# A graph layer and an expert layer in one kernel: wide products, ranks behind bursts, last scatters behind gathers, relation counts standing three times

## The reference

```
h   = layernorm(x)
red = segment_sum(h[src] + relvectors[edge_type], dst)
x   = x + gru_cell(red, h)          # gates r, z, n: 3 x 256 columns of w_ih and of w_hh
y   = layernorm(x)
top two of (y @ Wg + bg) pick experts; each: gelu(y @ W1 + b1) @ W2 + b2
x   = x + sum over the two picked experts
```

## Time and profile before

| | |
|---|---|
| median of three runs | 1621.61 us (1618.15 to 1624.96) |
| profiled execution, its own time | 1622.94 us |
| its span | 1621.1 us, mean granted TensorE clock 0.891 |
| busy: TensorE / its weight loads | 1343.6 us (83%) / 1159.2 us (72%) |
| busy: VectorE / ScalarE / POOL | 1093.0 (67%) / 707.3 (44%) / 1033.3 us (64%) |

### The profile page before, as it was taken

One profiled execution on the slowest core, in us unless ns is written; L12 is line 12 of the kernel. 1 busy time (PEld: TensorE's weight loads), 2 busy tenths in 40 slices (PEclk: granted clock), 3 DMA queues, 4 the chain that ended last, 5 costly groups with the idle time before them and its releaser, 6 DMA issues. The chain is left out here.

```text
span 1621.1 us, 39990 instructions
## 1 busy us (share of the span) xinstructions
PE 1343.6 (83%) x14228; PEld 1159.2 (72%) x14228; DVE 1093.0 (67%) x3967; ACT 707.3 (44%) x1538; POOL 1033.3 (64%) x948
## 2 busy tenths in 40 slices
PE   1169999999999999998898887775754799999991
PEld 1137787888878878777777776664644699999991
DVE  7856677777777777788888888943545555555550
ACT  6323344445455454443443332221212567776660
POOL 2177667677777776677777767777772255555552
PEclk8559999999999999999998998686766899999996
DMA  9676434444454554444444543346641465555556
GB/s 305 171 219 188 143 98 115 128 137 141 138 148 144 144 141 135 129 133 136 134 128 135 147 125 111 111 118 232 211 115 51 102 97 93 93 95 100 95 80 178
DMA packets 136167, 220.59 MB, mean 136 GB/s; under 512 B 27761, under 2 KB 101046, under 8 KB 134688
## 3 DMA queue, kind: packets, MB, share of 16 engines
q0 software_dynamic: 63872, 123.12, 31.1%
q1 hardware_dynamic: 72096, 94.84, 19.5%
HBM read 169.05 MB, written 57.76 MB: 140 GB/s over the span
## 5 line engine op out<-in xcount | busy, mean ns | idle before, releaser
L667 POOL DMA_INDIRECT ring<-h_table,idx x728 | 725.1, 996 | 328.0 <-issue 252.7
L780 ACT ACTIVATE amat<-P 128x300 f16<-128x300 f32 (+3 forms) x608 | 230.9, 427 | 434.9 <-PE P L1635 427.9
L1648 PE MATMUL P<-hs,amat 128*126 128x256 f16 (+4 forms) x2646 | 366.9, 287 | 0.0
L1648 PEld LDWEIGHTS P<-hs,amat 128*126 128x126 f16 (+4 forms) x2646 | 299.7, 140 | 7.1
L721 POOL DMA_INDIRECT out_rows<-yo,xrows x112 | 176.8, 1578 | 162.2 <-DVE yo L1520 110.6
L1136 DVE TENSOR_SCALAR cone<-iota,comb 128x294 f16<-128x294 f16 (+3 forms) x840 | 255.5, 307 | 0.0
L1135 DVE TENSOR_SCALAR lone<-iota,slo 128x128 f16<-128x128 f16 x840 | 221.4, 264 | 32.8 <-PE P L1630 32.4
L1630 PE MATMUL P<-cone,lone 128*128 128x294 f16 (+3 forms) x840 | 164.6, 291 | 41.4 <-ACT amat L780 27.3
L1511 DVE SCALAR_TENSOR_TENSOR gl<-gT,scales,gh 128x512 f16<-128x512 f32 x112 | 84.1, 751 | 127.0 <-ACT gh L904 127.0
L676 POOL DMA_INDIRECT expert_rows<-xrow,slots x100 | 122.5, 1225 | 58.1 <-DVE slots L1265 28.2
L1863 PE MATMUL P<-xh,w_all 128*128 128x256 f16 x896 | 157.8, 275 | 0.0
(11 more groups left out here) (239 smaller groups left out, 2661.8 us busy)
## 6 DMA issues: line engine op xcount, KB each, us to landing
raw<-in_L_ffn_W_dram SPq DMA_DIRECT2D x32, 512.0 KB
xrows<-expert_rows SPq DMA_DIRECT2D x56, 257.0 KB, 3.3
ring<-h_table,idx POOLq DMA_INDIRECT x728
w_parts<-parts SPq DMA_DIRECT2D x16, 512.0 KB, 6.5
w_all<-w_parts SPq DMA_DIRECT2D x8, 1024.0 KB, 19.1
h_in<-h_table SPq DMA_DIRECT2D x25, 250.0 KB
x<-in_x_dram SPq DMA_DIRECT2D x25, 250.0 KB
out_rows<-x SPq DMA_DIRECT2D x25, 250.0 KB
```

What stands on the lines that cost most here:

```text
L667: nc.gpsimd.indirect_dma_start(out=ring[:, r, j, :], out_offset=None, in_=h_dram, in_offset=bass.IndirectOffsetOnAxis(ap=idx[:, slot, g * ...
L780: nc.scalar.activation(amat[:, b % 2, :, s * aw:(s + 1) * aw], P[2 + g % 2][:, 0:HIS * aw].rearrange("p (h w) -> p h w", w=aw), ACT.Copy). ...
L1648: nc.tensor.matmul(to, amat[:, b % 2, hi, 0:used], hs[:, hi, part * D:(part + 1) * D], start=(hi == 0 and part == 0), stop=False)
```

## The change

- `relations`: a new tile `rel_rows` holds the three parts under each other (48 partitions); `onetype` and `ramp` hold the 16 types three times, so that counts and `cts` have 48 rows; 2 matmuls of 48 partitions stand for 6 of 16. SP fills `rel_rows` with 3 small DMAs, queued behind the load of the first `x1` and ahead of the `raw` loads; TensorE waits for them (`s_stack`) before its slot matmuls.
- `head_piece`: one matmul of 512 columns per row block for two of 256; high and low sums lie side by side, and `low_sums` adds the second half with one more operation.
- TensorE's list: `gate_hn`, `transpose_x2` and `rank` go behind the pieces and bursts of their half. ScalarE's `move_group` of the later bursts goes ahead of `high_x2`.
- POOL's list: no scatter is placed behind a step from 88 on. Of the 25 tiles only tile 21 changes its place: from behind step 89 to behind all gathers.
- Start: `group_f` is made ahead of the `comb` operations, the wait for the slot matmuls (`head_slots`) comes at the end of half 0, and `weight_max` starts two halves later. Two tiles swap their places in SBUF.

```diff
-        onetype = sb("onetype", [128, 2, SC, R], F16)
-        cts = sb("cts", [R, STEP_G * WIN], F16)
+        onetype = sb("onetype", [128, 2, SC, PARTS * R], F16)
+        cts = sb("cts", [PARTS * R, STEP_G * WIN], F16)
...
-            return h - 1 if 1 <= h <= WJOBS else None
+            return h - 3 if 3 <= h <= WJOBS + 2 else None
...
             sp.dma_start(x1[:, :, :], node_rows(x, 0)).then_inc(x_loaded, 16)
+            sp.wait_ge(s_parts, 1)
+            for part in range(PARTS):
+                sp.dma_start(rel_rows[part * R:(part + 1) * R, :], rels[:, part, :]).then_inc(s_stack, 16)
...
-                    while done < TILES and (BEGIN[done] + 11) // 2 + 2 <= n:
+                    while n < NS - 3 and (BEGIN[done] + 11) // 2 + 2 <= n:
...
+                    for g in groups_of(h)[len(bursts[0]):] if bursts else []:
+                        move_group(g)
                     for i in stage_of(h, 8):
                         high_x2(i)
-                    for g in groups_of(h)[len(bursts[0]):] if bursts else []:
-                        move_group(g)
...
-                nc.vector.tensor_tensor(s_l[0:used, :], P[1 + 3 * (b % 2)][0:used, 0:D], s_h[0:used, :], ALU.subtract).then_inc(a_low, 1)
+                link(nc.vector.tensor_tensor(s_l[0:used, :], P[1 + 3 * (b % 2)][0:used, 0:D], s_h[0:used, :], ALU.subtract))
+                nc.vector.tensor_tensor(s_l[0:used, :], P[1 + 3 * (b % 2)][0:used, D:PD], s_l[0:used, :], ALU.add).then_inc(a_low, 1)
...
-                for part in range(PARTS):
-                    for f in range(KT):
-                        nc.tensor.matmul(P[0][:, f * STEP_G * WIN:(f + 1) * STEP_G * WIN], rels[:, part, f * 128:(f + 1) * 128],
-                                         cts[:, :], start=(part == 0 and f == 0), stop=False)
+                for f in range(KT):
+                    nc.tensor.matmul(P[0][:, f * STEP_G * WIN:(f + 1) * STEP_G * WIN], rel_rows[:, f * 128:(f + 1) * 128],
+                                     cts[:, :], start=(f == 0), stop=False)
...
-                    for part in range(2):
-                        nc.tensor.matmul(to, amat[:, b % 2, hi, 0:used], hs[:, hi, part * D:(part + 1) * D],
-                                         start=(hi == 0 and part == 0), stop=False)
+                    nc.tensor.matmul(both, amat[:, b % 2, hi, 0:used], hs[:, hi, :], start=(hi == 0), stop=False)
...
+                pe.wait_ge(s_stack, 16 * PARTS)
                 pe.wait_ge(s_groups, 16 * (len(ZONES) + 1) + 1)
...
                     if bursts:
                         head_burst(bursts[0])
-                    for i in stage_of(h, 8):
-                        transpose_x2(i)
-                    for i in stage_of(h, 11):
-                        rank(i)
                     if s == 0 and n < NS:
                         sums(n)
...
-                    for i in stage_of(h, 1):
-                        gate_hn(i)
...
                         if m + 1 < len(bursts):
                             head_burst(bursts[m + 1])
+                    for i in stage_of(h, 1):
+                        gate_hn(i)
+                    for i in stage_of(h, 8):
+                        transpose_x2(i)
+                    for i in stage_of(h, 11):
+                        rank(i)
```

More of the change, by code:

```diff
@@ L256, in shape_constants @@
     ident = np.eye(128, dtype=np.float32)
-    ramp = np.tile(np.concatenate([np.arange(WIN), np.arange(R), np.zeros(128 * len(WIDTHS))]).astype(np.float32), (128, 1))
+    ramp = np.tile(np.concatenate([np.arange(WIN), np.tile(np.arange(R), PARTS), np.zeros(128 * len(WIDTHS))]).astype(np.float32), (128, 1))
     for n, aw in enumerate(WIDTHS):
-        ramp[:, WIN + R + 128 * n:WIN + R + 128 * (n + 1)] = np.arange(128)[None, :] // aw == np.arange(128)[:, None]
+        ramp[:, WIN + PARTS * R + 128 * n:WIN + PARTS * R + 128 * (n + 1)] = np.arange(128)[None, :] // aw == np.arange(128)[:, None]
     iota = np.tile(np.arange(IOTA).astype(np.float16), (128, 1))
@@ L300, in gnn_ffn_kernel @@
         ident16 = sb("ident16", [128, 128], F16)
-        ramp = sb("ramp", [128, WIN + R])
+        ramp = sb("ramp", [128, WIN + PARTS * R])
         iota = sb("iota", [128, IOTA], F16)
@@ L310, in gnn_ffn_kernel @@
         rels = sb("rels", [R, PARTS, D], BF16)
+        rel_rows = sb("rel_rows", [PARTS * R, D], BF16)
         wg = sb("wg", [128, KT, NE])
@@ L428, in gnn_ffn_kernel @@
         with ExitStack() as early:
-            to_slots = early.enter_context(nc.sbuf_tensor("to_slots", [GMAX, len(WIDTHS), 128], F32))
+            slo_i = early.enter_context(nc.sbuf_tensor("slo_i", [128, HEAD * GC], I16))
         cone = sb("cone", [128, BUFS, IOTA], F16)
@@ L436, in gnn_ffn_kernel @@
         acc = sb("acc", [128, KT, ACOLS])
+        with ExitStack() as early:
+            to_slots = early.enter_context(nc.sbuf_tensor("to_slots", [GMAX, len(WIDTHS), 128], F32))
         s_h = sb("s_h", [128, D], F32R)
@@ L530, in _ @@
             load_chunk(1)
-            sp.dma_start(to_slots[:, :, :], c_ramp[0:GMAX, WIN + R:].rearrange("p (w s) -> p w s", s=128)).then_inc(s_const, 16)
-            for to, a in ((ident, c_ident), (ramp, c_ramp[:, 0:WIN + R]), (iota, c_half[:, 0:IOTA]), (cols, c_cols[:, 0:NCOL])):
+            sp.dma_start(to_slots[:, :, :], c_ramp[0:GMAX, WIN + PARTS * R:].rearrange("p (w s) -> p w s", s=128)).then_inc(s_const, 16)
+            for to, a in ((ident, c_ident), (ramp, c_ramp[:, 0:WIN + PARTS * R]), (iota, c_half[:, 0:IOTA]), (cols, c_cols[:, 0:NCOL])):
                 sp.dma_start(to[:, :], a).then_inc(s_const, 16)
@@ L1105, in head_keys, with head_slots @@
                 for first, end, k, aw, size, c in zone_batches():
-                    r = slice(GC * first, GC * end)
-                    nc.vector.scalar_tensor_tensor(comb[:, r], comb[:, r], aw / 128.0, dst_t[:, r], ALU.mult, ALU.add)
                     ins = nc.vector.tensor_copy(group_f[0:size, c], group_i[0:size, c])
                 ins.then_inc(s_groups, 1)
+                for first, end, k, aw, size, c in zone_batches():
+                    r = slice(GC * first, GC * end)
+                    ins = nc.vector.scalar_tensor_tensor(comb[:, r], comb[:, r], aw / 128.0, dst_t[:, r], ALU.mult, ALU.add)
+                link(ins)
+            def head_slots():
                 dve.wait_ge(s_slots, 1)
@@ L1354, in fast @@
                         second_norm(i, ORDER[i])
+                    if h == 0:
+                        head_slots()
                     if pass1_at(h) is not None:
                         weight_max(pass1_at(h))
-                    if h == WJOBS + 1:
+                    if h == WJOBS + 3:
                         weight_tops()
-                    if h == WJOBS + 2:
+                    if h == WJOBS + 4:
                         weight_diag()
-                    if h == WJOBS + 3:
+                    if h == WJOBS + 5:
                         weight_scales()
@@ L1644, in head_piece @@
                         pe.wait_ge(a_added, b - 1)
+                both = P[1 + 3 * (b % 2)][0:used, :]
                 to = P[1 + 3 * (b % 2)][0:used, 0:D]
                 for hi in range(HI * (n * of + m) // (pieces * of), HI * (n * of + m + 1) // (pieces * of)):
-                    for part in range(2):
-                        nc.tensor.matmul(to, amat[:, b % 2, hi, 0:used], hs[:, hi, part * D:(part + 1) * D],
-                                         start=(hi == 0 and part == 0), stop=False)
+                    nc.tensor.matmul(both, amat[:, b % 2, hi, 0:used], hs[:, hi, :], start=(hi == 0), stop=False)
                 if n == pieces - 1 and m == of - 1:
```

20 lines of the change are left out of this document (10 added, 10 removed).

## The result

| | before | after |
|---|---|---|
| median of six runs | 1622.43 us (1618.15 to 1624.96) | 1613.63 us (1612.56 to 1622.13) |
| ratio to before, 95% interval | | 0.9954 [0.9931, 0.9976] |
| first / last gather issued | 72.0 / 1211.2 us | 73.4 / 1208.5 us |
| first slot matmul | 81.1 us | 96.4 us |

Faster by 0.46%, less than the 0.5% that the prediction took as the least to tell from no change, but with an interval that stays under 1; 1604 had been forecast. All ratios leave out executions over 1.5% above the fastest of their kernel, medians in us don't.

The account below looks back on a forecast made before the run. TensorE was taken to set the pace in most steps, POOL near steps 58 to 65 and 76 to 90; -11 - 6 + 2 - 7 + 4 + 1 - 6 + 5 = -18 us gave 1604 us, range for 8 in 10 1588 to 1627.

Parts of the forecast that it names:

- The premise, "a saving per step counts some 63 times": Gather stage: TensorE sets the pace in steps 1 to 57 and 66 to 74, so savings count 63 times, not 91.
- Relations, -11: TensorE's relation matmuls, 2 for 6: four starts fewer save 0.175 us a step, times 63, -11 us.
- Wide products, -6: TensorE's products, 512 columns for twice 256: 5.5 ns saved per pair, some 1130 pairs that count, -6 us.
- VectorE, +2: VectorE's larger onetype (+0.27 us a step) and one more 0.41 us operation in 27 batches: 0 to +8, +2 taken.
- Order, -7 + 4: TensorE's list: waits for h_l, mask and xrow shrink, -7 us (0 to -15); new slot waits cost +4 (0 to +17).
- Scatters, +1: POOL's list: later ranks make slots later for scatters; +1 us taken.
- the slower rival: POOL's scatters wait for later ranks and stop the gathers behind them, giving 1630 us; chance 0.15.
- Tail, -6: End of POOL's list: tile 21's four scatters go behind all gathers, so the last gather goes out earlier, -6 us.
- Start, +5: Slot matmuls wait for rel_rows, landing about 95 us, 14 us late; most is made good, +5 us taken.

Follow-up runs that it names:

- e16: Kernel after without the low half of the gathered rows in the products, 16 matmuls of 48 columns a step instead of 32: 1608.43 us, 0.9887 of before.
- e13: Kernel after, unchanged, run again as the yardstick: 1618.06 us, 0.9942 of before.
- e17: e14 with TensorE's and ScalarE's lists in the order of the kernel before: 1620.93 us, 0.9969 of before.
- e18: e17 with each burst's products as two matmuls of 256 columns again, without VectorE's extra addition per batch: 1618.17 us, 0.9951 of before.
- e15: Kernel after with each wide product split into four matmuls of 128 columns: 1633.84 us, 1.0043 of before.
- e14: Kernel after with the three copies into rel_rows issued early on ScalarE's queue instead of SP's: 1610.52 us, 0.9889 of before.

## Why the prediction was wrong, by its steps

- **The premise, "a saving per step counts some 63 times".** This is the step that failed. It took POOL's stops for proof that TensorE paces steps 1 to 57. e16 is the test: 0.4 us less per step, 37 us in all, give 9.6, where the premise has 26. TensorE is the pace of a step only until VectorE and ScalarE are. From e13 to e16 TensorE's idle time in steps 10 to 90 grew from 130 to 143 us, as waits for `amat`, `cone` and slots, and its time at the lower clock from 181 to 212 us, half of which is lost: 13 + 15 is about what didn't arrive. The change itself shows the same: steps 10 to 59 take 625.9 us before, 640.0 in after and 633.6 in e13. They gave nothing back, though TensorE's relations take 0.16 us less in each of them.
- **Relations, -11.** The saving on TensorE is real (0.16 us a step, 0.175 forecast), its passage wasn't: at one quarter, about -4. e17 and e18 fit that: with the old order, steps 12 to 59 take 611.7 and 607.8 us against 606.3 before, with 13.4 and 12.2 us of waits for h_l up to 810 us instead of 7.1. Relations were not run alone on a chip of this kind.
- **Wide products, -6.** Mis-sized: two starts of 256 columns are 109.0 ns apart over the whole trace, not the 112 that one group of 16 gave, so the line through the earlier trace rows had a fixed part twice too large (109.0 - 256 x 0.417 = 2.3). 2 x 109 - 216 = 2 ns is left, 2.6 us on TensorE, and nothing in the time (e18). The Trainium skill, "TensorE: Matmul & The Clock Gate", part 1 (the 56 ns question), has 2.5 ns a matmul; for 256 and 512 columns the trace agrees with that, and not with my 5.5. In e15, 128 columns with a weight load each leave more, 58 - 128 x 0.417 = 4.6 ns.
- **VectorE, +2.** 0.552 and 0.424 us, as forecast. Its effect was not tested by itself. In e17, which has the added work in the old order, TensorE waits for `cone` 9.9 us up to 1080, before 10.4, while its waits for h_l grew by 7. So the longer waits for `cone` in after (23.8) came with the order, and a few us of the missing ones may be VectorE's.
- **Order, -7 + 4.** Waits for h_l, mask and xrow did go up to 1080 us, and slots were waited for 11 times as forecast, but for 15.0 us (3.6 before; 4 more were forecast, bounds 0 and 17), up to 4.7 at once, not under 1; cone took most of the rest. The net, -6 to -8.5 without the collision, is nearer to -3 than its +-7 can tell apart.
- **Scatters, +1, and the slower rival.** 2.8 us of waits; the rival fell.
- **Tail, -6.** Right for POOL: from the first gather of step 89 to that of step 90 e13 needs 10.1 us, before 16.1. Not right to the end: from the last gather's issue to the experts' first product pass 58.9 us in e13, 58.8 in after and 58.7 in e14, before 56.7. So 4 of the 6 us reach the experts. How it came to 2 us more behind the last gather was not looked into.
- **Start, +5.** Landing was right: the slot matmuls begin at 96.4 in after and 98.4 in e13, 93 to 97 forecast. The size is nearly right too, for a reason that the prediction mixed. e13 begins its products 15.1 us late, is 1.7 behind before at step 10 and 4.7 at step 12, the savings of those steps included. But e14, without the late copies, has steps 0 to 10 8.0 us shorter as well: what was counted as making up for the late start was there to be had without it, and the late copies themselves cost 8 (e14 against e13). `weight_max` two halves later also takes: it puts the last of the weight scaling right ahead of tile 0's gates. VectorE's timeline of e13:

```profile
215.91 0.16 DVE L1297 COPY wpow<-P 128x3 f32<-128x3 f32 x1 [1.45 <-PE P L1758]
...
222.13 0.68 DVE L1218 SCALAR_TENSOR_TENSOR oT<-oT,rT 128x500 f32<-128x500 f32 x1
```

TensorE waits 2.3 us for that oT, and steps 10 to 12 take 22.7 us for 19.6. e14 has this too; before hadn't. e14 is 6.6 us ahead of before at step 10 and 9.7 at step 90.

In sum, with e14 and e17: tail -4 to -6, order -6 to -13, late copies +8, and all else (relations, wide products, VectorE, the rest of the start) together between -7 and +2, where -15 had been taken for relations, wide products and VectorE alone; a quarter of the 17 us that the first two take off TensorE is 4. Each measurement has +-3 to 6 us, each difference +-5 to 7, so these sizes are rough. That the whole still lies in the range for 8 in 10 says little for the terms, since the largest two of them hardly arrived.

## What to carry to other kernels

Ask not only who waits for the engine that is to be relieved, but how far behind it the next engine is: where its waits are many and short on two other engines, take out a known amount of its work and see what arrives. A small transfer that something at the very start waits for belongs on a queue of its own. When other transfers move at the same time as gathers, 1 or 2 us of phase can decide over 5; compare orders on traces, and on more than one, not on one time.

## What was not expected of the hardware

- 37 us off TensorE gave 9.6, 21 us added cost 15.8.
- The same kernel takes 1622 us in the first comparison, 1624 and 1626 on chips 5 and 10, and 2074 to 2084 on chips 6, 0 and 14, with the experts' stage alike; a change worth 0.5% on the ones is worth 7% on the others.
- Starts of 128, 256 and 512 columns at full clock: 58, 109 and 216 ns apart; at the lower level 107, 213 and 427, which is 0.834 ns a column with no fixed part left.
- With three transfers of SP's queue begun just ahead, a gather came late: in e17 7.2 us from the end of the last issue to the products, 2.7 in before, where they begin behind it.
